# Re-ordering the small steps inside a merged cross-attention and feed-forward pipeline

## The reference

```
h = layernorm(x + multihead(x, x, x, causal), ln1)
h = layernorm(h + multihead(h, ctx, ctx), ln2)          # 16 heads of 16 columns
h = layernorm(h + relu(h @ w1.T + b1) @ w2.T + b2, ln3) # 1024 hidden columns
out = gated_attention(h, ctx, mask) + h
```

## Time and profile before

| what | value |
|---|---|
| median of 3 runs | 1209.85 us (1206.68 to 1212.49) |
| profiled execution: time, span | 1202.8 us, 1201.1 us |
| mean granted TensorE clock | 0.867 of full speed |
| PE busy, share of span | 874.3 us, 73% |
| DVE, ACT, POOL busy | 685.8, 477.9, 424.2 us |
| merged stage | about 440 to 960 us |

### The profile page before, as it was taken

One profiled execution on the slowest core, in us unless ns is written; L12 is line 12 of the kernel. 1 busy time (PEld: TensorE's weight loads), 2 busy tenths in 40 slices (PEclk: granted clock), 3 DMA queues, 4 the chain that ended last, 5 costly groups with the idle time before them and its releaser, 6 DMA issues. The chain is left out here.

```text
span 1201.1 us, 20625 instructions
## 1 busy us (share of the span) xinstructions
PE 874.3 (73%) x7396; PEld 724.2 (60%) x7412; DVE 685.8 (57%) x1438; ACT 477.9 (40%) x932; POOL 424.2 (35%) x559
## 2 busy tenths in 40 slices
PE   0368999999974522767888888888888716968786
PEld 0346777777753422545777777776777716857665
DVE  1445777777773324555565566655545323677886
ACT  1014555455553222455555455545443112422222
POOL 1124666666753102234444444434444300000000
PEclk9989999999998666577899899989898958977786
DMA  4588767767510362432222222122000020001101
GB/s 88 179 175 152 167 138 139 152 141 142 129 33 19 67 127 67 103 83 53 52 65 57 51 49 49 49 49 49 1 2 1 1 68 18 1 2 34 35 26 44
DMA packets 56988, 85.87 MB, mean 71 GB/s; under 512 B 13760, under 2 KB 49984, under 8 KB 52288
## 3 DMA queue, kind: packets, MB, share of 16 engines
q1 hardware_dynamic: 54784, 84.13, 31.3%
q10 hardware_dynamic: 2112, 0.52, 0.3%
HBM read 59.15 MB, written 24.96 MB: 70 GB/s over the span
## 5 line engine op out<-in xcount | busy, mean ns | idle before, releaser
L1125 DVE TENSOR_REDUCE a_nm<-a_s 128x2 f32<-128x512 f32 (+1 forms) x192 | 129.1, 681 | 82.0 <-PE a_s L952 80.0
L776 POOL TENSOR_TENSOR c_hl<-c_hid,c_hh 128x256 fp32r<-128x256 f32 x128 | 94.0, 735 | 225.7 <-DVE c_hid L668 225.7
L1091 ACT ACTIVATE a_pT<-a_st 128x512 f32<-128x512 f32 x192 | 111.5, 594 | 108.3 <-PE a_st L973 106.7
L668 DVE TENSOR_SCALAR c_hid<-c_up,ff_b_col 128x256 f32<-128x256 f32 x128 | 60.4, 474 | 127.2 <-ACT c_hh L538 126.1
L437 PE MATMUL c_down<-fw,c_hh 128*128 128x256 f32 x512 | 128.1, 315 | 4.4 <-DVE res L676 4.3
L538 ACT ACTIVATE c_hh<-c_up,ff_b_col 128x256 fp32r<-128x256 f32 x128 | 60.2, 470 | 137.3 <-PE c_up L119 137.3
L437 PEld LDWEIGHTS c_down<-fw,c_hh 128*128 128x128 f32 x512 | 94.2, 204 | 28.1 <-issue 23.1
L119 PE MATMUL c_up<-c_fxh,fw 128*128 128x256 f32 x512 | 105.1, 299 | 1.5 <-DVE c_hid L668 1.5
L1234 POOL TENSOR_SCALAR_AFFINE_SELECT a_pT<-a_pT 128x256 f32<-128x256 f32 (+1 forms) x192 | 89.2, 482 | 27.9 <-ACT a_pT L1091 27.3
L598 DVE TENSOR_REDUCE c_nm<-c_s 128x5 f32<-128x385 f32 (+1 forms) x96 | 55.5, 578 | 61.3 <-PE c_s L370 61.1
L119 PEld LDWEIGHTS c_up<-c_fxh,fw 128*128 128x128 f32 x512 | 85.9, 207 | 3.7 <-DVE c_hid L668 2.9
(11 more groups left out here) (237 smaller groups left out, 2408.7 us busy)
## 6 DMA issues: line engine op xcount, KB each, us to landing
qk_parts<-a_parts SPq DMA_DIRECT2D x16, 768.0 KB, 3.6
a_sq<-qk_parts SPq DMA_DIRECT2D x16, 384.0 KB, 5.2
a_sk<-qk_parts SPq DMA_DIRECT2D x16, 384.0 KB, 6.9
q_parts<-c_parts SPq DMA_DIRECT2D x16, 384.0 KB, 2.4
c_sq<-q_parts SPq DMA_DIRECT2D x16, 384.0 KB, 5.0
a_x<-in_xT SPq DMA_DIRECT2D x16, 256.0 KB, 9.0
res<-in_x SPq DMA_DIRECT2D x16, 256.0 KB, 5.9
a_sq<-qk_parts SPq DMA_DIRECT2D x16, 256.0 KB, 7.3
```

The costliest lines, as they stand in the source:

```text
L668: nc.vector.tensor_scalar(hid[n % NHID][:], up[n % 2][:, 0:S], b1[:, m:m + 1], 0.0, ALU.add, ALU.max).then_inc(s_hid, 1)
L776: nc.gpsimd.tensor_tensor(hl[:, m, :], hid[n % NHID][:], f32(hh[:, m, :]), ALU.subtract).then_inc(s_hl, 1)
L1091: nc.scalar.activation(pT[g % NPT][:], st_ps[g % 2][:], ACT.Exp).then_inc(s_exp, 1)
L1125: nc.vector.tensor_reduce(nm[c % 2][:, QT * heads[0] + qt:QT * heads[-1] + qt + 1:QT], s_ps[g % 2][:].rearrange("p (h k) -> p h k", h=len( ...
```

## The change

The lags of the U and D tiles grow by four slots, `turn_h2` moves from slot 0 to slot 4, and steps of ScalarE, VectorE and GpSimd move to other slots or to another place within one. No instruction is added or taken away.

```
-    ST_LAG, AV_LAG, UP_LAG, DOWN_LAG = 10, 13, 34, 42
+    ST_LAG, AV_LAG, UP_LAG, DOWN_LAG = 10, 13, 38, 46
 turn_h:        +  atleast(pe, s_fxl, c - 6)
 turn_h2:       -  atleast(pe, s_res, min(c + 1, B))    +  pe.wait_ge(s_res, min(c + 2, B))
 project_out:   -  atleast(pe, s_fxl, c)                +  atleast(pe, s_fxl, c - 1)
 tensor, per slot
-                if s == 0:
-                    turn_h2(n - 4)
                 scores(n, s)
                 scores_turned(g - ST_LAG)
...
-                if s == 5:
-                    turn_h(n + 3)
+                if s == 4:
+                    turn_h2(n - 4)
                 values; down_tile
                 if s == 7:
+                    turn_h(n + 3)
                     turn_max(n)
 scalar, per slot
                 if s == 0:
-                    fx_high(n - 4)
                     shift_rows(n - 1)
                 exps(g - ST_LAG)
-                if s == 2:
+                if s == 0:
+                    x_high(n + 2)
+                if s == 3:
                     centred_scale(n + 3, z1, s_zr, s_z, t.rstd)
                 if s == 4:
                     part_one(n + 2)
-                    deviation(n - 3)
                 if s == 5:
-                    x_high(n + 3)
+                    fx_high(n - 4)
+                    part_two(n + 2)
                 if s == 6:
-                    part_two(n + 2)
                     centred_scale(n - 3, z2, s_z2r, s_z2, rstd2)
-                    o_high(n - 2)
                 if s == 7:
                     shift_high(n)
+                    o_high(n - 2)
                 hidden_high(g - UP_LAG)
+                if s == 4:
+                    deviation(n - 3)
 vector, per slot
                 if s == 0:
+                    turn_av(n - 2, 0)
                     shift_low(n - 1)
-                if s == 1:
+                if s == 4:
+                    turn_av(n - 2, 1)
+                if s == 6:
+                    feed_residual(n - 6)
                     fx_low(n - 4)
-                if s == 2:
-                    feed_residual(n - 6)
                 maxes(n, s)
                 if s == 1:
+                    x_low(n + 2)
+                if s == 2:
                     centred(n + 3)
                     turn_back(n - 2, 0)
-                if s == 2:
+                if s == 3:
                     residual(n - 3)
-                if s == 3:
                     moments(n - 3)
-                    feed_moments(n - 6)
-                    turn_av(n - 2, 1)
                 if s == 4:
                     remainder(n + 2)
                 if s == 5:
                     inverse(n - 3)
                     centred2(n - 3)
+                if s == 6:
                     turn_back(n - 2, 1)
-                if s == 6:
-                    x_low(n + 3)
                 if s == 7:
-                    turn_av(n - 1, 0)
+                    feed_moments(n - 6)
                 hidden(g - UP_LAG)
 gpsimd, per slot
-                if s == 0:
+                if s == 1:
                     scale(n - 2, 0)
-                if s == 2:
+                if s == 4:
+                    shifted_rows(n + 3)
+                if s == 5:
+                    scale(n - 2, 1)
                     keep(n - 4)
-                if s == 3:
-                    shifted_rows(n + 3)
-                if s == 4:
-                    scale(n - 2, 1)
+                if s == 6:
+                    part_three(n + 2)
                 if s == 7:
-                    part_three(n + 2)
+                    shifted_rows2(n - 3)
                     o_low(n - 2)
-                    shifted_rows2(n - 3)
                 hidden_low(g - UP_LAG)
```

More of the change, by code:

```diff
@@ L332, in turn_h @@
                 atleast(pe, s_res, c - 5)
+                atleast(pe, s_fxl, c - 6)
                 for kt in range(KT):
@@ L343, in turn_h2 @@
                 pe.wait_ge(s_xl, min(c + 7, B))
-                atleast(pe, s_res, min(c + 1, B))
+                pe.wait_ge(s_res, min(c + 2, B))
                 for kt in range(KT):
@@ L410, in project_out @@
                 pe.wait_ge(s_ol, c + 1)
-                atleast(pe, s_fxl, c)
+                atleast(pe, s_fxl, c - 1)
                 pe.wait_ge(s_xl, min(c + 6, B))
```

## The result

| | kernel before | changed kernel |
|---|---|---|
| median, all runs | 1211.21 us (8 runs) | 1223.88 us (1219.94 to 1230.04, 8 runs) |
| ratio, 95% interval | 1 | 1.0117 [1.0084, 1.0149] |
| span of the profiled execution | 1201.1 us | 1220.2 us |
| mean granted TensorE clock | 0.867 | 0.849 |

Run again beside experiments e7 and e8, the changed kernel gave 1.0095 [1.0058, 1.0132]. It is about 1% slower. The prediction had 1212 us in a range of 1192 to 1227, with 0.37 for slower.

What follows compares the result with a forecast made beforehand. The prediction took the merged stage to be bound by TensorE plus its waits. Steady periods +7, iterations 4 and 5 -6, fill -1 and drain +2 gave +2 us on 1209.85, so 1212 us, range 1192 to 1227.

Steps and rivals of the forecast that it cites:

- The old wait: TensorE before turn_h2, waiting for GpSimd's normalised rows: moving turn_h2 four slots later removes 4.06 us an iteration.
- The new wait in slot 6: TensorE waits 3.9 us: 1.4 before scores turned, the rest before D, behind ScalarE's table loads and feed_residual.
- The sign that would have refuted it: ScalarE's hidden_high of slot 5 starting less than 4 us after slot 5 begins.
- The lower bound: Slot 6 wait if ScalarE were never late: U, hidden_high, hidden and feed_residual alone leave 1.77 us.
- the missing cover: Slot 6 has no project_out or scores over the steps before D; before, project_out in slot 2 covered them.
- The new wait in slot 1: Value turn and low maxima at VectorE's head of slot 0 delay maxima and exponential: TensorE loses 1.6 us.
- The clock: The slot 6 wait keeps the 1.6 us low-clock penalty, as often as now: 1.8 us an iteration.
- The sum: Steady iteration: 21.7 + 3.9 + 1.6 = 27.2, plus 1.8 of clock, 29.0 us against 28.1; +7 over eight periods.
- The ends: Outside the steady periods: iterations 4 and 5 give -6 us, the fill -1, iterations from 14 on +2.
- rival C: Slot 1's 1.6 us wait brings its own low-clock stretch, two an iteration: +13 us, near 1226; chance 0.17.
- Rival B: Same waits, but the split slot 6 wait keeps the clock up, few low stretches: 1194 us; chance 0.18.

Runs made afterwards that it cites:

- e7: Changed kernel plus 6 matmuls nobody reads behind project_out in slot 2: 1231.43 us, ratio 1.0133 to the kernel before.
- e8: Changed kernel with VectorE's value turns back in slots 7 and 3 and the square root ahead of hidden_high: 1189.63 us, 0.9803 of the kernel before.
- e1: Changed kernel with the second layer norm's square root replaced by a copy, so no steady table switches: 1186.55 us, 0.9842 of the kernel before.
- e9: Changed kernel with D four slots behind U (DOWN_LAG 42), first D in slot 2 again, fx_low in slot 5: 1173.97 us, 0.9740 of the kernel before.
- e4: Changed kernel with unread matmuls in slot 6, 8 before the scores turned and 16 before the first D: 1190.66 us, 0.9870 of the kernel before.
- e2: Changed kernel with VectorE's two value turns back in slots 7 and 3: 1188.78 us, 0.9844 of the kernel before.
- e6: Kernel before with 34 matmuls nobody reads ahead of turn_h2: 1186.54 us, 0.9837 of the kernel before.
- e3: Changed kernel with the square root step ahead of hidden_high in slot 4 of ScalarE: 1203.27 us, 0.9962 of the kernel before.
- e5: Kernel before with GpSimd's shifted_rows2 moved from slot 7 to slot 6, ahead of hidden_low: 1127.46 us, 0.9344 of the kernel before.

## Why the prediction was right or wrong

*The old wait goes.* Right: `turn_h2` has no wait.

*The new wait in slot 6.* Right in place and cause, a little too long: 1.11 + 2.16 = 3.3 us against 3.9. The sign that would have refuted it did not come: `hidden_high` of slot 5 started 4.7 us after slot 5 began, not less than 4, and D started 6.4 us after, where 6.7 were reckoned. The lower bound was misjudged: the bare chain from U to D was put at 1.77 us, from the drain; e1 shows it at 2.2 us in steady state, so ScalarE's lateness adds 1.1 us, and not the 2.1 between 1.77 and 3.9. e9 shows that the cause is the missing cover, as the prediction's step had it.

*The new wait in slot 1.* Right in cause, too long: 0.74 us in most iterations and 1.33 where the clock had been high through slot 0, against 1.6. The forecast reckoned slots 7 and 0 at the high clock; most often slot 7 and the first third of slot 0 ran at the low one and so took longer, which hid part of the wait.

*The clock.* This is the step that failed, in size. It said that the 3.9 us keep the penalty "as often as now", 1.8 us an iteration. Measured were 72 us at the low clock in eight periods, 65 of them with TensorE busy: 8.1 us an iteration, a cost of 4.1 us. It was read from how often a wait is followed by a low stretch, and the length of a stretch was taken over from before. The e4 run, which keeps the wait's length and takes away the low clock, shows that the low clock is what the wait costs there.

*The sum.* A steady iteration was forecast as 21.7 + 5.5 of waits + 1.8 of clock = 29.0 us and came as 21.7 + 4.3 + 4.1 = 30.1. The two errors have opposite signs, -1.2 and +2.3 us an iteration; that the forecast missed by only 12 us, and that its range held, owes something to this luck. +7 for the steady periods became +16.

*The ends.* From the first `turn_h` to the last D the profiles show 496.9 us before and 514.7 after (514.3 in the second profile of the changed kernel), +18. Of that +16 are the steady periods, -3 the fill (126.7 to 123.9 us, up to the first of the nine `turn_max`), which was put at -7, and +5 the drain (145.1 to 150.3 us from the last of them), which was put at +2. So the ends gave +2 and not -5. The whole moved by +13 us in the medians instead of +2.

*The rivals.* A period over 30 us was named as the sign of rival C, and C's 1226 is near the measured 1224, but by another road: it put a second stretch behind the slot 1 wait, and the profile has instead one stretch that is mostly three times as long, begins in the slot 6 wait and ends before slot 1 begins. C's premise is not idle, though: where slot 6 leaves the clock up, as in e9, the waits of slot 1 do bring a stretch of their own, in every second iteration. Rival B's claim that a split wait keeps the clock up fell: 1.1 and 2.16 us brought it down in each of the eight periods. Only with the 2.16 us gone, in e9, did the 1.1 us of slot 6 leave it at 1.00.

*What stays open.* Why the stretch is 10.2 us in the changed kernel and 3.4 us in e1 and e2, with nearly the same D wait in front (2.16 to 2.22 us) and the same matmuls behind it. In e1 the 1.1 us before it are gone, but in e2 they are even 1.43. Undoing any one part shortened it, more work in slot 2 (e7) shortened it in steady state and not over the whole stage, and undoing two parts (e8) made it longer than undoing one (e2). No run told one cause apart.

## What to carry to other kernels

Before a pipeline is lengthened to hide a wait, look in the list of the engine that is late: here the late step stood behind two others in one slot while that engine was idle in the slot before, and moving one line gave 6.6%, where the longer lag gave a loss. A wait that a step shared with a long neighbour comes back as soon as the step is moved from under it, so for each moved step ask what covered it. And where TensorE is the bound, sum its time at the low clock beside its waits: two orders of the same steps with nearly equal waits (4.3 and 4.0 us an iteration, the changed kernel and e2) lay 33 us apart.

## What the runs showed of the hardware

The clock stayed at 1.2 GHz for up to 10.2 us, the last 9 of them with matmuls back to back, and a wait filled with unread matmuls kept it at 2.4 GHz in all but one of the eight steady periods (e4) or in all of them (e6). That alone was worth 30 us in the changed kernel (e4) and 20 us in the kernel before (e6), 2.4% and 1.6% for no useful work. In the orders without a fill or other added work, a steady period less its waits and less half of its busy low-clock time is 21.5 to 22.2 us, whatever the order (before, changed, e1, e2, e3, e5, e8, e9). The pattern of long and short stretches repeated in the same iterations in two executions of one kernel.
